# The two FFNs of a three-layer hybrid: where the routing coefficients are multiplied in, and how far the down product follows

## The reference

```python
coef = jnp.zeros((T, E), topk_w.dtype).at[jnp.arange(T)[:, None], topk_idx].add(topk_w)
g = jnp.einsum('th,ehi->tei', x, Wg)
u = jnp.einsum('th,ehi->tei', x, Wu)
h = jax.nn.silu(g) * u * coef[:, :, None]
moe_out = jnp.einsum('tei,eih->th', h, Wd)
shared = jax.nn.silu(x @ SWg) * (x @ SWu) @ SWd
```

## Time and profile before

| what | value |
|---|---|
| median of 3 runs | 1341.8 us (1339.83 to 1342.63) |
| the profiled execution | 1334.83 us, its span 1333.1 us |
| PE busy in the span | 1022.0 us (77%), 5292 matmuls |
| VectorE busy | 1020.5 us (77%) |
| ScalarE busy | 731.1 us (55%) |
| POOL busy | 324.2 us (24%) |
| mean granted clock of PE | 0.759 of full speed |
| first FFN, first silu to last silu | 436.3 to 711.8 us |
| second FFN, first silu to last silu | 1048.5 to 1321.3 us |

### The profile page before, as it was taken

One profiled execution on the slowest core, in us unless ns is written; L12 is line 12 of the kernel. 1 busy time (PEld: TensorE's weight loads), 2 busy tenths in 40 slices (PEclk: granted clock), 3 DMA queues, 4 the chain that ended last, 5 costly groups with the idle time before them and its releaser, 6 DMA issues. The chain is left out here.

```text
span 1333.1 us, 17448 instructions
## 1 busy us (share of the span) xinstructions
PE 1022.0 (77%) x5292; PEld 720.6 (54%) x5292; DVE 1020.5 (77%) x1712; ACT 731.1 (55%) x878; POOL 324.2 (24%) x217
## 2 busy tenths in 40 slices
PE   4655567766652999999997836777763699999997
PEld 2333344434332777787775423443443577777776
DVE  4447988888638899999998755455437799999997
ACT  2324999999941555555554313333432355555554
POOL 2002555555510222222222310000000122222221
PEclk8665555555555999999998855555595799999999
DMA  1000000000000666666662000000000466666664
GB/s 47 0 0 1 1 0 1 0 1 1 0 7 8 145 151 149 149 148 147 146 141 56 1 0 0 1 0 1 1 7 9 89 150 149 149 149 149 149 149 100
DMA packets 26089, 85.24 MB, mean 64 GB/s; under 512 B 3904, under 2 KB 17088, under 8 KB 17856
## 3 DMA queue, kind: packets, MB, share of 16 engines
q1 hardware_dynamic: 26048, 84.70, 27.6%
HBM read 82.58 MB, written 2.10 MB: 64 GB/s over the span
## 5 line engine op out<-in xcount | busy, mean ns | idle before, releaser
L1041 ACT ACTIVATE sg<-ps 128x512 f32<-128x512 f32 x264 | 157.9, 599 | 123.9 <-PE ps L430 123.8
L1047 ACT ACTIVATE hh<-hf 128x512 fp32r<-128x512 f32 x264 | 167.1, 633 | 106.7 <-DVE hf L1656 106.4
L430 PE MATMUL ps<-xh,whi 128*128 128x512 f32 x528 | 206.8, 392 | 0.0
L430 PE MATMUL ps<-xh,wlo 128*128 128x512 f32 x528 | 206.7, 391 | 0.0
L430 PE MATMUL ps<-xl,whi 128*128 128x512 f32 x528 | 206.5, 391 | 0.0
L1650 DVE TENSOR_TENSOR hl<-hf,hh 128x512 fp32r<-128x512 f32 x264 | 185.9, 704 | 26.7 <-ACT hh L1047 6.8
L1145 POOL TENSOR_TENSOR rr<-xr,rr 128x2048 f32<-128x2048 f32 x32 | 144.8, 4546 | 211.5 <-ACT xr L933 207.3
L1656 DVE TENSOR_TENSOR hf<-h,cbc 128x512 f32<-128x512 f32 x256 | 195.3, 763 | 0.0
L1643 DVE TENSOR_TENSOR h<-sg,ps 128x512 f32<-128x512 f32 x264 | 179.3, 679 | 15.6 <-ACT sg L1041 7.1
L1189 POOL CAST whi<-wraw 128x384 fp32r<-128x384 f32 x66 | 61.8, 936 | 478.6 <-PE ps L430 375.1
L1485 DVE TENSOR_REDUCE mx<-ps 128x4 f32<-128x1024 f32 x64 | 78.4, 1224 | 71.3 <-PE ps L430 71.3
(11 more groups left out here) (246 smaller groups left out, 1585.3 us busy)
## 6 DMA issues: line engine op xcount, KB each, us to landing
cbc<-routing_coefficients SPq DMA_DIRECT2D x128, 512.0 KB, 5.9
wraw<-in_wexp_dram SPq DMA_DIRECT2D x66, 192.0 KB, 5.9
X<-in_x_dram SPq DMA_DIRECT2D x4, 256.0 KB, 4.7
routing_coefficients<-cT SPq DMA_DIRECT2D x8, 128.0 KB, 2.3
out_dram<-X SPq DMA_DIRECT2D x4, 256.0 KB, 2.9
cstb<-in_consts_dram SPq DMA_DIRECT2D x1, 648.0 KB, 3.5
wa<-in_wA_dram SPq DMA_DIRECT2D x1, 256.0 KB, 4.1
wb<-in_wB_dram SPq DMA_DIRECT2D x1, 192.0 KB, 3.6
```

The costliest lines, as they stand in the source:

```text
L430: return pe.matmul(o, l, r, start=start, stop=stop, **kw)
L1041: act.activation(sg[c % 2][:, :], bank(4 + 2 * (c % 2)), ACT.Silu).then_inc(s_sg, 1)
L1047: act.activation(hh[c][:, :], hf[c % 2][:, :], ACT.Copy).then_inc(s_hh, 1)
```

## The change

The coefficients are multiplied into silu(gate) by GpSimd: cg = sg * cbc. VectorE's multiplication with up in PSUM then gives hf at once, and its third operation goes. A unit of PE is followed by the down product of the unit three before (`LAG`), hh and hl are made of the unit two before, and sg, cg, hf are rings of four. The split weights have four slots; wraw and cbc keep two. GpSimd splits the weights of a pair between its second and third product of the pair before, and the weights of the first pair ahead of its first product. SP waits for cg instead of hf before it overwrites cbc. The loops run over four pairs a turn instead of two.

```diff
-CR_WS, CR_HL, CR_H, CR_YD = 1, 2, 1, FF_STEPS
+CR_WS, CR_CG, CR_HL, CR_H, CR_YD = 1, 3, 3, 3, 3 * FF_STEPS
+LAG = 3
...
-            whi = [sb(f"whi{s}", [P, 3 * P], F32R) for s in range(2)]
-            wlo = [sb(f"wlo{s}", [P, 3 * P], F32R) for s in range(2)]
+            whi = [sb(f"whi{s}", [P, 3 * P], F32R) for s in range(4)]
+            wlo = [sb(f"wlo{s}", [P, 3 * P], F32R) for s in range(4)]
...
-            sg = [sb(f"sg{s}", [P, FF_TOK]) for s in range(2)]
-            h1 = [sb(f"h1{s}", [P, FF_TOK]) for s in range(2)]
-            hf = [sb(f"hf{s}", [P, FF_TOK]) for s in range(2)]
+            sg = [sb(f"sg{s}", [P, FF_TOK]) for s in range(4)]
+            cg = [sb(f"cg{s}", [P, FF_TOK]) for s in range(4)]
+            hf = [sb(f"hf{s}", [P, FF_TOK]) for s in range(4)]
...
-                        sp.wait_ge(s_h, i * (2 * FF_STEPS) + (s0 + s * FF_STEPS + CR_H))
+                        sp.wait_ge(s_cg, i * (2 * FF_STEPS) + (s0 + s * FF_STEPS + CR_CG))
...
                 def y(n, slot, chunk):
 
-                    pe.wait_ge(s_hl, n + CR_HL)
+                    pe.wait_ge(s_hl, n + (1 + CR_HL))
...
-                    for b, read, done in ((0, s_sg, s_g), (1, s_h1, s_u_)):
+                    for b, done in ((0, s_g), (1, s_u_)):
                         if not first:
-                            pe.wait_ge(read, n - 1)
+                            if b == 0:
+                                pe.wait_ge(s_sg, n - 1)
+                            else:
+                                pe.wait_ge(s_h, n + (CR_H - 1))
...
-                with pe.Fori(0, PAIRS // 2) as i:
-                    for s in range(2):
-                        pe.wait_ge(s_ws, i * 2 + (w0 + 2 + s + CR_WS))
+                with pe.Fori(0, PAIRS // 4) as i:
+                    for s in range(4):
+                        pe.wait_ge(s_ws, i * 4 + (w0 + 2 + s + CR_WS))
                         for c in range(FF_STEPS):
-                            n = i * (2 * FF_STEPS) + (s0 + (s + 1) * FF_STEPS + c)
+                            n = i * (4 * FF_STEPS) + (s0 + (s + 1) * FF_STEPS + c)
                             gate_up(n, s, c, False)
-                            y(n - 1, s if c >= 2 else 1 - s, (c - 2) % FF_STEPS)
+                            y(n - LAG, s if c >= LAG else (s - 1) % 4, (c - LAG) % FF_STEPS)
...
-                def silu(n, c, sg_used):
+                def silu(n, c):
                     act.wait_ge(s_g, n + 1)
-                    if sg_used is not None:
-                        act.wait_ge(s_h1, sg_used)
-                    act.activation(sg[c % 2][:, :], bank(4 + 2 * (c % 2)), ACT.Silu).then_inc(s_sg, 1)
+                    act.wait_ge(s_cg, n + (CR_CG - 3))
+                    act.activation(sg[c][:, :], bank(4 + 2 * (c % 2)), ACT.Silu).then_inc(s_sg, 1)
...
-                            silu(n, c, n - 1)
-                            high(n, (c - 1) % FF_STEPS)
+                            silu(n, c)
+                            high(n - 2, (c - 2) % FF_STEPS)
...
-                with pool.Fori(0, PAIRS // 2) as i:
-                    for s in range(2):
-
-                        pool.wait_ge(s_yd, i * (2 * FF_STEPS) + (s0 + s * FF_STEPS + CR_YD))
-                        split(s, i * 2 + (w0 + 2 + s), i * 16 + 16 * (loads[s] + 1))
+
+                def weigh(n, c, coefs):
+
+                    pool.wait_ge(s_sg, n + 1)
+                    pool.wait_ge(s_h, n + (1 - FF_STEPS + CR_H))
+                    pool.tensor_tensor(cg[c][:, :], sg[c][:, :], coefs, ALU.mult).then_inc(s_cg, 1)
+
+                def split_pair(i, s):
+
+                    pool.wait_ge(s_yd, i * (4 * FF_STEPS) + (s0 + (s - 2) * FF_STEPS + CR_YD))
+                    split(s % 2, s, i * 4 + (w0 + 2 + s), i * 32 + 16 * (s // 2 + loads[s % 2] + 1))
+
+                def pairs(i, last):
+                    for s in range(4):
+                        for c in range(FF_STEPS):
+                            n = i * (4 * FF_STEPS) + (s0 + (s + 1) * FF_STEPS + c)
+                            if c == 0:
+                                pool.wait_ge(s_cl[s % 2], i * 64 + (16 * PAIRS * f + 32 * (s // 2) + 32))
+                            weigh(n, c, cbc[s % 2][:, c * FF_TOK:(c + 1) * FF_TOK])
+                            if c == 1 and s < 3:
+                                split_pair(i, s + 1)
+                            if c == 1 and s == 3 and not last:
+                                split_pair(i + 1, 0)
+
+                split_pair(0, 0)
+                for c in range(FF_STEPS):
+                    weigh(s0 + c, c, one_s[:, :])
+                with pool.Fori(0, PAIRS // 4 - 1) as i:
+                    pairs(i, False)
+                pairs(PAIRS // 4 - 1, True)
...
                 def gate_up(n, c):
 
-                    dve.wait_ge(s_sg, n + 1)
+                    dve.wait_ge(s_cg, n + (1 + CR_CG))
                     dve.wait_ge(s_u_, n + 1)
-                    dve.tensor_tensor(h1[c % 2][:, :], sg[c % 2][:, :], bank(5 + 2 * (c % 2)), ALU.mult
-                                      ).then_inc(s_h1, 1)
+                    dve.wait_ge(s_hl, n + (1 - FF_STEPS + CR_HL))
+                    dve.tensor_tensor(hf[c][:, :], cg[c][:, :], bank(5 + 2 * (c % 2)), ALU.mult).then_inc(s_h, 1)
...
-                def weigh(n, c, coefs):
-
-                    dve.wait_ge(s_h1, n + 1)
-                    dve.wait_ge(s_hl, n - 1 + CR_HL)
-                    dve.tensor_tensor(hf[c % 2][:, :], h1[c % 2][:, :], coefs, ALU.mult).then_inc(s_h, 1)
...
-                            low(n, (c - 1) % FF_STEPS)
-                            if c == 0:
-                                dve.wait_ge(s_cl[s], i * 32 + (16 * PAIRS * f + 32))
-                            weigh(n, c, cbc[s][:, c * FF_TOK:(c + 1) * FF_TOK])
+                            low(n - 2, (c - 2) % FF_STEPS)
...
```

More of the change, by code:

```diff
@@ L311, in hybrid @@
         s_sg = sem("silu_ready")
-        s_h1 = sem("gate_up_ready")
+        s_cg = sem("gate_weighed")
         s_h = sem("h_ready")
@@ L818, in experts @@
                 for c in range(FF_STEPS):
[L819 to L824 removed]
+                    gate_up(s0 + c, 3, c, c < 2)
+                    if c >= LAG:
+                        y(s0 + c - LAG, 3, c - LAG)
+                with pe.Fori(0, PAIRS // 4) as i:
+                    for s in range(4):
+                        pe.wait_ge(s_ws, i * 4 + (w0 + 2 + s + CR_WS))
                         for c in range(FF_STEPS):
[L826 removed]
+                            n = i * (4 * FF_STEPS) + (s0 + (s + 1) * FF_STEPS + c)
                             gate_up(n, s, c, False)
[L828 removed]
+                            y(n - LAG, s if c >= LAG else (s - 1) % 4, (c - LAG) % FF_STEPS)
                 end = s0 + (PAIRS + 1) * FF_STEPS
[L830 to L831 removed]
+                for c in range(FF_STEPS - LAG, FF_STEPS):
+                    y(end - FF_STEPS + c, 3, c)
                 for c in range(FF_STEPS):
@@ L1183, in samples_b, with split @@
                                    ).then_inc(s_pbx, 1)
-            def split(slot, n, loaded):
-                pool.wait_ge(s_wl[slot], loaded)
+            def split(raw, slot, n, loaded):
+                pool.wait_ge(s_wl[raw], loaded)
                 pool.sem_inc(s_mark, 1)
-                pool.tensor_copy(whi[slot][:, :], wraw[slot][:, :]).then_inc(s_whi, 1)
+                pool.tensor_copy(whi[slot][:, :], wraw[raw][:, :]).then_inc(s_whi, 1)
                 pool.wait_ge(s_whi, n)
-                pool.tensor_tensor(wlo[slot][:, :], wraw[slot][:, :], whi[slot][:, :],
+                pool.tensor_tensor(wlo[slot][:, :], wraw[raw][:, :], whi[slot][:, :],
                                    ALU.subtract).then_inc(s_ws, 1)
@@ L1208, in prepare_experts @@
                 pool.memset(one_s[:, :], 1.0).then_inc(s_z, 1)
-                split(1, (PAIRS + 1) * f + 1, 16 * ((PAIRS // 2 + 1) * f + 1))
+                split(1, 3, (PAIRS + 1) * f + 1, 16 * ((PAIRS // 2 + 1) * f + 1))
+            pool.sem_inc(s_cg, CR_CG)
             pool.sem_inc(s_ws, CR_WS)
@@ L1646, in low @@
                 def low(n, c):
[L1648 to L1658 removed]
+                    dve.wait_ge(s_hh, n + 1)
@@ L1659, in experts @@
+                    dve.wait_ge(s_yd, n + (1 - FF_STEPS + CR_YD))
+                    dve.tensor_tensor(hl[c][:, :], hf[c][:, :], hh[c][:, :], ALU.subtract).then_inc(s_hl, 1)
                 for c in range(FF_STEPS):
                     gate_up(s0 + c, c)
-                    if c >= 1:
-                        low(s0 + c, c - 1)
-                    weigh(s0 + c, c, one_s[:, :])
-                with dve.Fori(0, PAIRS // 2) as i:
-                    for s in range(2):
+                    if c >= 2:
+                        low(s0 + c - 2, c - 2)
@@ L1666, in experts @@
+                with dve.Fori(0, PAIRS // 4) as i:
+                    for s in range(4):
                         for c in range(FF_STEPS):
```

(10 more changed lines are left out.)

25 lines of the change are left out of this document (11 added, 14 removed).

## The result

The changed kernel takes 1507.1 us (median of 4 runs, 1505.74 to 1507.81) against 1340.84 (4 runs): a ratio of 1.1238, interval 1.1221 to 1.1256. The profiled execution took 1507.38 us with a span of 1505.6.

A forecast was written before the change was run, and what follows sets the result against it. Bound by a hand-over chain through POOL's product, lengthened by the split, instead of PE's 2.04 us a unit. FFN middles 155.7, starts 9.8 and ends 1.0 sum to 166.5 us; added to median 1341.8: 1508 us, range about 1450 to 1590.

The forecast's parts named there:

- The chain: From hl(n-3)'s end through y, gate, silu, POOL's product and hf to hl(n-1)'s end: 5.07 us for two units, 2.53 each.
- The one price with no row, POOL to VectorE: Hand-over from POOL's product to VectorE's hf: between 0.03 and 0.24 us, taken as 0.07.
- The split: POOL's cast and wlo between products of units 1 and 2: a quartet takes 10.86 us instead of 10.12.
- the rival in which hl gets in first: hl(-1) goes ahead of wlo: 11.8 us a quartet, 59 us more, 1567 us; chance 0.24.
- 31 quartets x 10.86: Units 4 to 131 of an FFN: plus 3 x 2.53 makes 344.3 us, +76.5 and +79.2 over before.
- the loops of half as many turns: Loops over four pairs a turn instead of two: counted as nothing.
- The start: First pair's split ahead of POOL's first product: silu(4) at 448.97 instead of 444.03, +4.9 us in each FFN.
- The ends: Last silu's start to last y in each FFN: 4.60 us instead of 4.11, +0.5 each.
- the forecast 166.5: Total added time in us over both FFNs: 155.7 between units 4 and 131, 9.8 starts, 1.0 ends.
- That the clock falls for good: PE, busy some 75%, drops to half clock: units at least 3.87 us, kernel 1803 us; chance 0.06.
- That PE becomes the bound: Chain takes no more than 4.08 us for two units, y never waits: 1338 us; chance 0.06.

The follow-up runs named there:

- Run 3: Changed kernel with POOL copying silu(gate) instead of multiplying it by the coefficients: 1424.6 us, ratio 1.066 to the kernel before.
- run 2: Changed kernel with the down product four units behind instead of three: 1388.5 us, ratio 1.039 to the kernel before.
- Run 4: Changed kernel with weights split only for the first five pairs of an FFN, old weights afterwards: 1466.3 us, ratio 1.098 to the kernel before.
- run 9: Changed kernel with the coefficient product back on VectorE and the down product four units behind: 1316.3 us, ratio 0.9843 to the kernel before.
- run 10: Changed kernel, four units behind, splits only for the first pairs, hl(n-2) ahead of hf(n) on VectorE: 1338.9 us, ratio 1.0003 to the kernel before.
- run 11: As run 10, but hl subtracts hh from up in PSUM instead of from hf in SBUF: 1329.4 us, ratio 0.9941 to the kernel before.
- run 1: Changed kernel with hl(n-2) ahead of hf(n) on VectorE, nothing else: 1397.8 us, ratio 1.045 to the kernel before.
- run 5: Changed kernel with the down product four units behind and no splits after the first five pairs of an FFN: 1358.0 us, ratio 1.016 to the kernel before.
- Run 8: Changed kernel with the coefficient product back on VectorE, still three units behind, rings, slots and loops kept: 1336.8 us, ratio 1.0002 to the kernel before.
- Run 6: Changed kernel, four units behind, cast behind a quartet's first product and wlo behind its third: 1370.3 us, ratio 1.024 to the kernel before.
- run 7: As run 6, with an FFN's first split behind the second product instead of ahead of the first: 1361.5 us, ratio 1.019 to the kernel before.
- run 12: As run 7, with hl ahead of hf on VectorE, product on POOL and all splits made: 1349.0 us, ratio 1.009 to the kernel before.

## Why the prediction was right, and where it was lucky

**The chain.** Forecast 5.07 us for two units; undisturbed units take 2.47 + 2.57 = 5.04. Its steps measured: hl's end to silu 1.76 (1.75), silu and hand-over 0.68 (0.68), product and hand-over to VectorE 1.33 (1.34), hf 0.60 (0.61), hl 0.68 (0.69). The one price with no row, POOL to VectorE, was taken as 0.07 and is 0.03, while the product is 1.29 to 1.30 instead of 1.27; they cancel. The 1.11 estimated by the Trainium skill (GPSIMD Engine Reference, "Elementwise — side-by-side cycle accounting") does not agree with these rows. Run 3 shows that the product stands in the chain, run 2 that the chain was what bound.

**The split.** Counted from 561.29, the start of the product of unit 1, the cast ends at 1.74, wlo runs from 1.82 to 2.83, hl ends at 3.38, the product of unit 2 at 4.52, and the next product starts at 5.82; no step is off by more than 0.03, and the quartet is the forecast 10.86. wlo did lead hl, by 0.11, so the rival in which hl gets in first did not come about. Run 4 gives the split's price: it leaves out 27 of the 31 splits between units 4 and 131 of an FFN, 54 x 0.74 = 40 us by the prediction, and 41 were measured (37.8 of them between these units in the profiles). The run's own forecast counted 26, for 38.

**What failed.** Three terms of the sum were off, though small.

- "31 quartets x 10.86", with "the loops of half as many turns" at nothing: three of four quartets take 10.84 to 10.91, the fourth, where the loops turn, 11.09. At 0.25 each, 7 turns are 1.8 us in an FFN. That is the excess in the first (1.9) and over half of it in the second (3.1). The other 1.3 there lie in its first two quartets (23.2 us from unit 4 on, against 22.0 in the first FFN): a long hl leaves PE idle for 1.90 us, and from 1150.30 to 1153.69 its matmuls follow by 0.43 us, at half clock (0.51 over 1150.2 to 1153.2). No run takes this apart further.

```profile
1148.78 0.50 PE L431 MATMUL ps<-hh,whi 128*128 128x512 f32 x1 [1.90 <-DVE hl L1680]
...
1151.16 0.63 PE L431 MATMUL ps<-xh,wlo 128*128 128x512 f32 x1
```

- The start, "+4.9, and I take the same in the second FFN": the first came out right by two errors. The matmuls of up and gate were taken at full clock; PE had stood idle for 5.5 us, from 443.06 they followed at half clock (0.50 over 443 to 447), and silu of unit 3 came at 446.03 instead of 444.72. That let hl(0) in ahead of the product of unit 3, so that it ran in 0.69 where the prediction had it blocked, which made good for the delay. The second start cost 3.0.
- The ends, "+0.5 each", cost 1.9 and 2.1. In both, PE had idled for 1.56 us ahead of the last three y (798.26 and 1495.03), and most of their matmuls followed by 0.43 us, again at half clock (0.50 over 798.9 to 801.9 and 1495.0 to 1498.4). The prediction had the last y start as soon as the last hl was done, 4.60 us behind the last silu; it started 5.33 and 5.64 behind it.

These make the 6.0 us by which the span's growth, 172.5, exceeds the forecast 166.5. That the median, 1507.1, lies within 1 us of 1508 is luck: the profiled execution of before was 6 us under its median, that of the changed kernel was not. On the profiles' own scale the forecast was 1501 and the time 1507.4. The range would have held either.

**The other rivals.** That the clock falls for good did not come about: 1.00 in the middle of the first FFN, 0.99 in the second; it fell for some 3 to 4 us at a time at the starts and the ends. That PE becomes the bound needed the chain under 4.08 us; units of PE's 2.04 came about only with other chains: in run 9, and in runs 10 and 11 once the splits had stopped.

**The later expectations** failed more often than the prediction. Runs 1, 2 and 5 each forecast PE's 2.04 and met the next wall: first the split and the products behind it, which make hf late, then hl held by the product. Run 8's forecast of some 1326 overlooked that the split draws out hl wherever the product stands. Run 6 came out above its range, run 9 below, and the control, run 10, 19 us below the time that it was to keep. Runs 3, 4, 7, 11 and 12 held; in run 12 the forecast came from adding up, over a quartet, the time that can't run side by side.

## What to carry to other kernels

An engine that looks idle is not a free place for a step of a chain: count the whole round from a result back to itself in hand-overs, and compare it with the round of the bound engine, times the units that lie between. Where two engines shut each other out, add up what both do in one period as if it were one engine, and look at who comes second by how much. If a wait is to be hidden, first let the consumer follow further behind; that, with the work left where it was, gave the 1.6% here, on top of longer rings and more slots, which by themselves changed nothing.

## What was not expected of the hardware

- An operation that is shut out by another engine can fall into step with it and pay in every unit: hl had a median of 1.59 us instead of 0.69 between 500 and 700 us of run 5, where the sum of undisturbed times (1.29 + 0.69 us) fits into a unit of 2.04.
- A turn of the loop is not free for a chain. The first three hf of every turn of 16 units start some 0.2 us after the product's end, all others in the middle of an FFN 0.03. Here it is 0.21 (493.24 + 1.29 to 494.74); the hl behind that hf was still at work when the next product began, and that product took 1.54:

```profile
493.24 1.29 POOL L1207 TENSOR_TENSOR cg<-sg,cbc 128x512 f32<-128x512 f32 x1 [1.35 <-ACT sg L1044]
...
494.74 0.69 DVE L1674 TENSOR_TENSOR hf<-cg,ps 128x512 f32<-128x512 f32 x1 [1.53 <-POOL cg L1207]
495.35 0.68 DVE L1680 TENSOR_TENSOR hl<-hf,hh 128x512 fp32r<-128x512 f32 x1
...
495.63 1.54 POOL L1207 TENSOR_TENSOR cg<-sg,cbc 128x512 f32<-128x512 f32 x1 [1.10 <-ACT sg L1044]
```

- PE's pause of 5.5 us at the start of the first FFN was followed by a granted clock of 0.76 over 436 to 450 us, where the kernel before had 1.00 in the same stretch (the row here). Pauses of 1.0 us once a quartet cost no clock: 1.00 from 450 to 690 us. But after the 1.90 us ahead of 1148.78, and after the 1.56 ahead of the last y of each FFN, matmuls at half clock followed.

```profile
436.00:450.00 14.00, 12.85 (x54) 9.39 (x53) 12.22 (x19) 8.00 (x14) 4.53 (x4) 1.00 0.71 169
```
